# Layer 2's scan: the drives of two states in one GpSimd instruction, and thirteen states of every 32 weighed by GpSimd

## The reference, cut to what matters

```
dt = softplus(dts + dt_proj_b)
def step(h, inp):
    dt_l, u_l, B_l, C_l = inp
    dA = jnp.exp(dt_l[..., None] * A)
    h = h * dA + (dt_l * u_l)[..., None] * B_l[:, :, None, :]
    y = jnp.einsum('bkdn,bkn->bkd', h, C_l)
    return (h, y)
```

## Time and profile before

| | |
|---|---|
| device time, median of 3 runs | 39439.33 us (39406.36 to 39439.39) |
| the profiled execution's own time | 39424.39 us |
| its span, first to last instruction | 39422.3 us |
| POOL busy | 30996.9 us (79%) |
| DVE busy | 33863.2 us (86%) |
| PE busy | 28993.4 us (74%) |
| ACT busy | 20028.1 us (51%) |
| mean granted PE clock | 0.882 of full |

### The profile page before, as it was taken

The page is one execution under the profiler, slowest core; times in us unless marked ns, Lnnn a source line. Parts: engine busy times, 40 slices in busy tenths (PEclk is TensorE's granted clock), DMA queues, the critical chain, the costliest instruction groups (busy, mean ns, idle before and its releaser), DMA issues. The chain is left out here.

```text
span 39422.3 us, 270979 instructions
## 1 busy us (share of the span) xinstructions
PE 28993.4 (74%) x61476; PEld 11456.5 (29%) x61476; DVE 33863.2 (86%) x33757; ACT 20028.1 (51%) x37861; POOL 30996.9 (79%) x14776
## 2 busy tenths in 40 slices
PE   7777777777777777777777777777777777777777
PEld 3232232322323223232232322323223232232322
DVE  8969889698896988969889698896988969889698
ACT  4545545455454554545545455454554545545455
POOL 6949869498694986949869498694986949769497
PEclk8888888888888888888888888888888888888888
DMA  3424334243342433424334243342433424334243
GB/s 112 151 92 152 133 110 151 91 152 134 109 151 91 151 135 110 151 92 152 133 110 151 92 152 132 111 151 91 152 132 110 151 92 152 132 110 152 92 152 132
DMA packets 1387318, 5029.10 MB, mean 128 GB/s; under 512 B 164273, under 2 KB 165817, under 8 KB 1381441
## 3 DMA queue, kind: packets, MB, share of 16 engines
q1 hardware_dynamic: 1385536, 5010.20, 36.6%
HBM read 4938.25 MB, written 71.30 MB: 127 GB/s over the span
## 5 line engine op out<-in xcount | busy, mean ns | idle before, releaser
L664 PE MATMUL PS<-WORK,CST 128*128 128x512 f32 x36096 | 19786.3, 693 | 8394.2 <-POOL WORK L558 7532.9
L547 POOL TENSOR_TENSOR WORK<-WORK,XN 128x1024 f32<-128x1024 f32 x8192 | 19215.6, 2375 | 1.3
L664 PEld LDWEIGHTS PS<-WORK,CST 128*128 128x128 f32 x36096 | 7517.5, 220 | 20984.1 <-POOL WORK L558 10357.1
L1036 ACT ACTIVATE PS<-WORK,AN 128x512 f32<-128x512 f32 x17408 | 11307.1, 679 | 1970.7 <-DVE WORK L1577 1088.6
L1569 DVE TENSOR_TENSOR_SCAN PS<-PS,HST,WORK 128x512 f32<-128x512 f32 x8960 | 10971.6, 1271 | 45.4 <-ACT PS L1036 32.1
L1569 DVE TENSOR_TENSOR_SCAN WORK<-PS,HST,WORK 128x512 f32<-128x512 f32 x5376 | 6582.9, 1266 | 0.0
L558 POOL TENSOR_TENSOR WORK<-WORK,CWIDE 128x1024 f32<-128x1024 f32 x2048 | 4847.2, 2367 | 134.0 <-issue 81.0
L1036 ACT ACTIVATE HST<-PS 128x2 f32<-128x2 f32 x5152 | 858.1, 167 | 6590.3 <-DVE WORK L1577 6154.3
L1577 DVE TENSOR_TENSOR WORK<-PS,WORK 128x1024 f32<-128x1024 f32 x3072 | 3762.9, 1225 | 105.1
L634 POOL MEMSET XN<- 128x66 f32 x32 | 4.9, 153 | 4122.2 <-DVE SM L1423 4023.5
L1036 ACT ACTIVATE WORK<-PS,DTB 128x512 f32<-128x512 f32 x2304 | 1554.8, 675 | 2174.8 <-DVE WORK L1537 1658.6
(11 more groups left out here) (155 smaller groups left out, 24336.3 us busy)
## 6 DMA issues: line engine op xcount, KB each, us to landing
XN<-xbc_rows SPq DMA_DIRECT2D x4096, 512.0 KB, 3.7
WORK<-xbc_rows SPq DMA_DIRECT2D x2816, 512.0 KB, 4.3
CWIDE<-xbc_rows SPq DMA_DIRECT2D x2304, 512.0 KB, 4.3
BIG<-in_spec_dram SPq DMA_DIRECT2D x32, 2048.0 KB, 12.2
X<-in_x_dram SPq DMA_DIRECT2D x68, 512.0 KB, 4.8
xbc_rows<-WORK SPq DMA_DIRECT2D x512, 64.0 KB, 3.1
out_dram<-X SPq DMA_DIRECT2D x64, 512.0 KB, 5.0
xbc_rows<-WORK SPq DMA_DIRECT2D x128, 32.0 KB, 1.6
```

Of the source, the lines that this page charges most:

```text
L547: nc.gpsimd.tensor_tensor(S.both(S.Q[u % 6]), S.both(S.DU[u // SN % 2]), S.wide(S.BW, u).unsqueeze(1).to_broadcast([P, 2, NT]), MUL).then_ ...
L664: return nc.tensor.matmul(o, w, r, start=start, stop=stop)
L1036: return nc.scalar.activation(o, i, f, **k)
```

## The change

Two things change in layer 2's scan.

`make_drive`, one unit of 2 x 512 columns, becomes `make_drives`, two units of together 4 x 512 columns. It is called at even units only, for units u + 2 and u + 3, where `make_drive` was called at every unit for u + 3. It writes two neighbouring buffers of Q, waits until both are free (as before, the unit three before the current one must be summed), and raises the semaphore `drive` by two when it ends. There is one instruction for the two units.

The states that POOL weighs are now counted over 32 units: 1, 4, 6, 9, 12, 14 in the even groups, as before, and 17, 19, 21, 24, 26, 28, 30 in the odd groups, that is states 1, 3, 5, 8, 10, 12 and 14. DVE weighs 19 of 32 in place of 20. The scans of the units that changed hands write to Q instead of PSUM.

```diff
--- before.py
+++ after.py
@@ -24,7 +24,7 @@
 RANK = 8
 GROUPS = 32
 POOL_STATES3 = (2, 5)
-POOL_STATES = (1, 4, 6, 9, 12, 14)
+POOL_STATES = (1, 4, 6, 9, 12, 14, 17, 19, 21, 24, 26, 28, 30)
 
 
 def shape_constants():
@@ -288,7 +288,7 @@
 
             def on_pool(s, u):
 
-                return u % SN in s.pool
+                return u % (2 * SN) in s.pool
 
             def weighed_by_pool(s, u):
 
@@ -318,6 +318,11 @@
             def wide(s, bufs, u):
 
                 return bufs[u // 2 % 4][:, NT * (u % 2):NT * (u % 2 + 1)]
+
+            def two(s, u):
+
+                at = 2 * NT * (u % 6)
+                return WORK[:, at:at + 4 * NT].rearrange("p (n d l) -> p n d l", n=2, d=2)
 
             def loads(s, u):
 
@@ -537,16 +542,16 @@
                     nc.gpsimd.tensor_tensor(S.like(S.DU[g % 2], g), S.like(S.DT[g % 2], g), S.cols(BIG1, g),
                                             MUL).then_inc(S.du_ready, 1)
 
-                def make_drive(u):
+                def make_drives(u):
 
                     if u % SN == 0:
                         e.wait_ge(S.du_ready, u // SN + 1)
                     e.wait_ge(S.b_loaded[u // 2 % 4], S.loads(u))
                     if u >= 6:
-                        e.wait_ge(S.summed, u - 5)
-                    nc.gpsimd.tensor_tensor(S.both(S.Q[u % 6]), S.both(S.DU[u // SN % 2]),
-                                            S.wide(S.BW, u).unsqueeze(1).to_broadcast([P, 2, NT]),
-                                            MUL).then_inc(S.drive, 1)
+                        e.wait_ge(S.summed, u - 4)
+                    rows = S.BW[u // 2 % 4].rearrange("p (n l) -> p n l", n=2)
+                    nc.gpsimd.tensor_tensor(S.two(u), S.both(S.DU[u // SN % 2]).unsqueeze(1).to_broadcast([P, 2, 2, NT]),
+                                            rows.unsqueeze(2).to_broadcast([P, 2, 2, NT]), MUL).then_inc(S.drive, 2)
 
                 def weigh(u):
 
@@ -561,8 +566,7 @@
                 sum_dt(0, 0)
                 sum_dt(0, 1)
                 make_du(0)
-                for u in range(3):
-                    make_drive(u)
+                make_drives(0)
                 for u in range(S.units):
                     g, n = u // SN, u % SN
                     if g + 1 < KDIR * NCH:
@@ -572,8 +576,8 @@
                             sum_dt(g + 1, 1)
                         if n == 12:
                             make_du(g + 1)
-                    if u + 3 < S.units:
-                        make_drive(u + 3)
+                    if u % 2 == 0 and u + 2 < S.units:
+                        make_drives(u + 2)
                     if S.on_pool(u):
                         weigh(u)
```

## The result

The changed kernel takes 40724.62 us (median of 4 runs, 40718.03 to 40745.1) against 39439.36 us before: ratio 1.0326, 95% interval 1.0311 to 1.0342. The forecast was 40800 us. The profiled execution has a span of 40743.2 us, 1320.9 more than before.

A forecast was written before the change was run, and what follows sets the result against it. POOL was taken to set the pace, DVE pulled along. Walking two groups start to start gave 256 x 5.6 = +1434 us, edges -60, on 39424.39: 40798, said as 40800 us, 80% range 40350 to 41350.

The forecast's parts named there:

- busy time alone: POOL's work over two groups: 112.4 us after against 112.8 before, so by busy time nothing happens.
- a long instruction that costs much less than two: Rival on POOL's pair of drives: at 3.7 us or less the kernel gets faster, floor 38700 us; chance 4%.
- as much as U's rows: Rival on POOL's pair of drives: it costs 5.64 us, like make_du's strided rows, giving 44300 us; chance 4%.
- The order: Layer 2's scan: later drives make POOL and DVE stop in turn, +6.1 us per two groups in columns, +5.1 in rows.
- W19: POOL's weighing of unit 19, odd group: POOL waits 1.27 us ahead of it.
- the first S: POOL's first sum_dt of a group, needing DVE's log_small: waits 2.0 us in odd groups, 1.2 in even.
- W4: POOL's weighing of state 4, even group: waits 0.8 us for its scan.
- D(6,7): POOL's drive pair for units 6 and 7: short wait for PE's sum, hidden by state 4's weighing waiting 0.8 us.
- W9: POOL's weighing of state 9, even group: waits 1.3 us for ACT's carry behind the second softplus.
- PE's pace: Rival: PE is slow when state 14's weighing ends, delaying take_y in all groups, +1380, 42180 us; chance 5%.
- The rows and the edges: Row directions: +5.1 us per two groups. Edges together: -60 us, including +35 for the first scan of each image.
- The other two: Edge terms: shorter scans in a direction's first chunk, -64 us; no S and U waits in an image's last group, -32.

The follow-up runs named there:

- Experiment 1: Changed kernel with each long drive instruction replaced by two single drives in its place, new table kept: 40659.32 us, ratio to before 1.0311.
- 2: Changed kernel with the old weighing table (POOL weighs twelve of 32 states), pairs of drives kept: 40096.27 us, ratio to before 1.0169.
- 3: Kernel before with only the weighing table changed to thirteen of 32, single drives in their old places: 40005.95 us, ratio to before 1.0146.
- 7: Changed kernel with make_du at state 12 issued behind the pair of drives (14,15) instead of ahead: 40676.29 us, ratio to before 1.0313.
- 8: Changed kernel with POOL weighing state 10 instead of state 9 in the even groups: 40420.43 us, ratio to before 1.0251.
- 10: Changed kernel with the old weighing table and sum_dt of state 8 issued behind the pair of drives (10,11): 40115.69 us, ratio to before 1.0176.
- experiment 5: Changed kernel with old table, single drives for states 10 and 11, pair (12,13) ahead of state 9's weighing: 39360.22 us, ratio to before 0.9983.
- experiment 6: Kernel of experiment 5 with the pair of drives (8,9) ahead of state 4's weighing instead of behind it: 40285.4 us, ratio to before 1.0214.

## Why the prediction was right

**What bounds, and busy time alone.** Right: POOL's busy time stayed (+65 us), and the pair costs 4.48 us, taken at 4.49 from two shorter shapes. The bound from above, U's 2 x 2.82, had no part in it, and the rivals of a long instruction that costs much less than two, or as much as U's rows, fall with that number.

**The order.** Right in place and size for the odd group: W19 waits 1.24 (walked 1.27), the first S 2.06 (2.0), 60.72 us for the group (60.66). Experiment 1 shows that the places cost as much without the long instruction, experiments 2 and 3 what the pairs and the table cost apart. That POOL's waits and not DVE's are the ones to count was said in the walk ("POOL is alone"). It rests on three runs: DVE's waits for drives fell to 934 us with the time unchanged (experiment 1), its longest wait moved with the time unchanged (7), and one gap of POOL's went together with its own size in time (8).

**The even group.** Right in sum (58.33, walked 58.3), by one wait exchanged for another: I had W4 wait 0.8 for its scan and D(6,7) wait a little inside that. In the trace D(6,7) waits 0.89 for PE, and W4 not at all, since POOL now comes to it just after its scan is ready. The prediction had named this wait but not sized it; that it is as long as the 0.8 that it replaces is luck. S waits 1.05 (1.2), W9 1.22 (1.3). That W9's wait is on the path is shown by experiments 8 and 10.

**PE's pace.** The rival in which PE is slow behind W14 did not come about:

```profile
1045.12 5.85 PE L668 MATMUL PS<-WORK,CST 128*128 128x512 f32 x8 [7.21 <-POOL WORK L563]
1051.90 3.70 PE L668 MATMUL PS<-WORK,CST 128*128 128x512 f32 x8 [0.92 <-POOL WORK L563]
```

The eight matmuls behind the weighing of state 14 took 3.70 us as before; at the pace of those ahead of it two groups would have taken over 4 us more. PE's mean granted clock did fall, from 0.89 to 0.86 and 0.85 over a group, but take_y starts at 1055.63, 3.83 us behind the end of W30, as it did before (3.84).

**The rows and the edges.** These are the terms that were mis-sized, by 53 us together of 1374. Counting DVE's 32 scans per group through the trace gives the length of every two groups, as a mean of the 16 images:

| two groups | before | after | more | walked |
|---|---|---|---|---|
| column directions, steady | 112.88 | 119.06 | +6.18 | +6.1 |
| rows forwards, steady | 111.03 | 116.07 | +5.04 | +5.1 |
| rows backwards, steady | 111.06 | 115.75 | +4.69 | +5.1 |
| first two groups, k = 0 | 111.49 | 114.03 | +2.54 | |
| last two of an image, to the last scan | 106.57 | 107.31 | +0.74 | |

The steady groups alone would give 256 x 5.52 = 1414 us, where the walk had 1434: the backward rows were dearer in the walk, which had taken them as the forward ones. The span grew by 1320.9, so the edges are worth -93, and I had -60. One part of them was right; an image's first scan waited 8.42 us where it had waited 6.21, 2.2 more:

```profile
350.68 2.35 DVE L1573 TENSOR_TENSOR_SCAN PS<-PS,WORK 128x512 f32<-128x512 f32 x2 [8.42 <-POOL WORK L553]
```

The other two were too small. At the start of three of the four directions two groups grew by some 2 us less than in the steady run, and by 1.4 more in the backward rows. The largest edge is the end of an image: its last two groups grew by 0.74, where a steady pair of groups taken to its last scan grew by 5.4; the walk took off only 2 us for the S and U that are not there. Some 2.8 us per image came back outside layer 2's scan, which is within the scatter of that part. Why each edge has its size was not tried by a run.

**What stays open.** The cause of the backward rows' 0.4 us and of each edge, and the few us per image by which the part outside layer 2's scan differs between kernels.

## What to carry to other kernels

When two engines are both nearly full and work for each other, the sum of busy times tells neither the sign nor the size of a change to their order; walk one period with start-to-start times and put every wait in, ACT's small copies and PE's sum too. Joining the instructions of two units puts the first result where the second stood: behind whatever stood between the two, and behind the second unit's work as well. Before doing so, see how long each result lay ready before it was used, and put a long instruction under each latency instead of behind it. The engine that waits longest need not be the one that loses: moving its longest wait left the time as it was, and filling a shorter one of the engine whose work ends the period took off just its size.

## What was not expected of the hardware

A POOL multiplication of 2 x 2 x 512 columns with both inputs broadcast over a dimension costs what its columns cost, 4.48 us against 2 x 2.31: 0.14 us saved, so this kernel had little to win by longer instructions. And a weighing put 4.5 us later left PE idle for 5.98 us instead of 1.33, after which its granted clock was 0.50 for 3.4 us; with the same instructions on POOL's list the kernel was 2.3% slower than that of experiment 5 (experiment 6).
